# ViT tower kernel: the third channel's loads of the first sixteen image chunks move from SyncE's DMA queue to ScalarE's

## The reference, cut to what matters

```python
patches = X.reshape(B, C, N_PATCHES, PATCH, N_PATCHES, PATCH)
patches = patches.transpose(0, 2, 4, 1, 3, 5).reshape(B, N_PATCHES * N_PATCHES, IN_D)
tokens = jnp.einsum('bpi,hi->bph', patches, W) + b
...
h = _L0_tok_ref(x, ...)
h = h + _L0_attn_ref(_layernorm(h), ...)     # 512 positions at a time share weights and a moving average
h = h + _L0_ffn_ref(_layernorm(h), ...)      # each expert takes its 1024 best tokens
```

## Time and profile before

| | us |
|---|---|
| median of 3 runs | 994.54 |
| lowest, highest | 993.32, 994.76 |
| the profiled execution | 988.4 |
| its span, first to last instruction | 986.6 |
| TensorE busy | 756.6 (77% of the span) |
| ScalarE busy | 446.5 (45%) |
| VectorE busy | 556.1 (56%) |
| GpSimd busy | 477.7 (48%) |

### The profile page before, as it was taken

The page is one execution under the profiler, slowest core; times in us unless marked ns, Lnnn a source line. Parts: engine busy times, 40 slices in busy tenths (PEclk is TensorE's granted clock), DMA queues, the critical chain, the costliest instruction groups (busy, mean ns, idle before and its releaser), DMA issues.

```text
span 986.6 us, 9758 instructions
## 1 busy us (share of the span) xinstructions
PE 756.6 (77%) x2896; PEld 396.9 (40%) x2896; DVE 556.1 (56%) x1238; ACT 446.5 (45%) x730; POOL 477.7 (48%) x488
## 2 busy tenths in 40 slices
PE   0168489999999999999999995625128899788771
PEld 0123235544544554454445543414114455344330
DVE  0210157778778877877787777592687543231110
ACT  0634357656665775666566522321253132222220
POOL 2233444555545554645555322261110768888885
PEclk9778789999999999999999996856556799899896
DMA  9699998898889889888988111000010233343432
GB/s 224 155 207 212 199 208 203 195 217 192 207 196 218 195 206 218 198 191 200 217 191 197 49 31 34 21 12 11 22 14 1 47 53 63 63 66 63 66 38 27
DMA packets 135681, 126.39 MB, mean 128 GB/s; under 512 B 17605, under 2 KB 126013, under 8 KB 135501
## 3 DMA queue, kind: packets, MB, share of 16 engines
q1 hardware_dynamic: 113600, 91.27, 40.1%
q0 software_dynamic: 19488, 33.51, 18.0%
q10 hardware_dynamic: 2540, 0.99, 0.5%
HBM read 87.99 MB, written 12.98 MB: 102 GB/s over the span
## 4 chain that ended last, share of the span: by engine, by line
PE 25%; DVE 24%; POOL 20%; issue 15%; DMA 8%; ACT 5%; SPq 2%; ACTq 1%; DVEq 0%; POOLq 0%
PE bank L1352 10%; POOL out L620 9%; POOL XS L610 6%; DMA XS<-in_x 5%; DVE Y L966 4%; PE bank L1450 3%; DVE stats L916 3%; DVE O L908 3%; DVE XR L908 2%; DVE QT L1041 2%; ACT XS L819 2%; POOL rsB L492 2%; PE bank L1435 2%; PE bank L1481 2%; SPq L421 2%
## 5 line engine op out<-in xcount | busy, mean ns | idle before, releaser
L1352 PE MATMUL bank<-XS,WT 126*128 126x512 f32 (+1 forms) x608 | 313.2, 651 | 33.9 <-DMA XS<-XS 33.9
L801 ACT ACTIVATE XS<-XS 84x1152 f32<-84x1152 f32 (+1 forms) x192 | 187.6, 1027 | 34.7 <-DMA XS<-in_x 32.5
L1352 PEld LDWEIGHTS bank<-XS,WT 126*128 126x128 f32 (+1 forms) x608 | 113.2, 195 | 169.7 <-issue 168.8
L567 POOL COPY XS<-XS 84x1152 f32<-84x1152 f32 x64 | 89.0, 1390 | 82.1 <-DMA XS<-in_x 79.1
L620 POOL DMA_INDIRECT out<-XS x64 | 103.3, 1614 | 26.6 <-issue 18.6
L580 POOL DMA_DIRECT2D XS<-XS x128 | 71.3, 560 | 56.0 <-PE bank L1352 41.1
L610 POOL DMA_INDIRECT XS<-token_rows,XS x64 | 65.0, 1016 | 47.8 <-DVE XS L1244 28.6
L966 DVE TENSOR_TENSOR_SCAN Y<-qdec,XT 128x512 f32<-128x512 f32 (+1 forms) x68 | 78.5, 1175 | 8.4 <-ACT XT L688 8.4
L848 ACT ACTIVATE XS<-bank,VT 128x512 f32<-128x512 f32 x64 | 44.0, 687 | 66.8 <-PE bank L1562 66.8
L1562 PE MATMUL bank<-XS 128*128 128x512 f32 x128 | 69.5, 693 | 1.4 <-ACT XS L688 0.8
L972 DVE SCALAR_TENSOR_TENSOR ET<-Y,ema_c,ET 128x512 f32<-128x512 f32 (+1 forms) x68 | 61.7, 907 | 1.8
(11 more groups left out here) (236 smaller groups left out, 1289.3 us busy)
## 6 DMA issues: line engine op xcount, KB each, us to landing
XS<-in_x SPq DMA_DIRECT2D x192, 392.0 KB
XS<-XS POOLq DMA_DIRECT2D x128, 189.0 KB, 7.6
out<-O SPq DMA_DIRECT2D x16, 256.0 KB, 6.7
token_rows<-XR SPq DMA_DIRECT2D x16, 256.0 KB, 6.9
XS<-in_L_ffn_W SPq DMA_DIRECT2D x16, 256.0 KB, 3.1
XS<-in_L_tok_W SPq DMA_DIRECT2D x1, 1176.0 KB, 9.3
XS<-token_rows,XS POOLq DMA_INDIRECT x65, 2.6
out<-XS POOLq DMA_INDIRECT x64
```

The costliest lines, as they stand in the source:

```text
L567: pool.tensor_copy(ST[0:ROWS, n % 2, :, :, :].rearrange("p m j r -> p m r j"), px[:, :, :, PASSES:PATCH])\
L801: ins = act.activation(area(slice(0, ROWS), k // 4, piece, m0, m0 + CCOL // 2).rearrange("p m j r -> p m r j"), px[:, :, :, REST * piece:m ...
L1352: ins = pe.matmul(TOK[half][:, :], WT[rows, t, :], area(rows, half, t // REST)[:, :, t % REST, :], start=(t == 0), stop=(t == PASSES - 1))
```

## The change

SyncE issues only channels 0 and 1 of chunks 0 to 15 (`SHARED` is 16), and all three channels of the later ones. ScalarE issues channel 2 of chunks 0 to 15: chunk 0's ahead of all its small loads, chunks 1's and 2's behind them, and chunk `n + 3`'s right behind the last piece of its copy of chunk `n` (for `n` from 0 to 12), after waiting for `copied(n)` and `staged(n)`. The semaphores and their counts stay. The two helpers that build the access patterns move out of SyncE's function.

```diff
+        SHARED = 2 * CHUNKS
...
             def load_chunk(n):
 
                 if n < CHUNKS * NP:
-                    for c in range(C):
+                    for c in range(C - 1 if n < SHARED else C):
                         sp.dma_start(raw(n, c), rows_of(n % CHUNKS, n // CHUNKS, c)).then_inc(load[n % RING].sem, 16)
...
+            def load_last(n):
+
+                act.dma_start(raw(n, C - 1), rows_of(n % CHUNKS, n // CHUNKS, C - 1)).then_inc(load[n % RING].sem, 16)
+
+            load_last(0)
             for v, row, n in vectors:
...
             act.dma_start(lnb[:, :], bass.AP(ln_b.tensor, 0, [[0, 128], [1, D]])).then_inc(c_loaded.sem, 16)
+            for n in range(1, RING):
+                load_last(n)
...
                 if piece == C - 1:
                     ins.then_inc(copied.sem, 1)
+                    if n + RING < SHARED:
+                        act.wait_ge(*copied.done(n))
+                        act.wait_ge(*staged.done(n))
+                        load_last(n + RING)
```

More of the change, by code:

```diff
@@ L406, in run, with rows_of, raw @@
                 iteration(NP, ((None, group(NP - 1, 1)),), False, False)
+        def rows_of(k, hy, c):
+            return x[CHUNK * k:CHUNK * k + CHUNK, c, ds(hy * PATCH, PATCH), :].rearrange("b p w -> p b w")
+        def raw(n, c):
+            return RAW[c:ROWS:C, n % RING, :].rearrange("p (b w) -> p b w", b=CHUNK)
+        SHARED = 2 * CHUNKS
         @block.sync
         def _(sp):
[L411 to L415, removed]
             def load_chunk(n):
                 if n < CHUNKS * NP:
-                    for c in range(C):
+                    for c in range(C - 1 if n < SHARED else C):
                         sp.dma_start(raw(n, c), rows_of(n % CHUNKS, n // CHUNKS, c)).then_inc(load[n % RING].sem, 16)
```

## The result

| | before | after |
|---|---|---|
| median, same chip in turn (10 executions each) | 993.39 us (991.54 to 995.22) | 988.42 us (986.33 to 990.83) |
| ratio, 95% interval | | 0.9946 (0.9933 to 0.9959) |
| profiled execution, its span | 988.4, 986.6 us | 987.64, 985.9 us |

The change makes the kernel 5.0 us faster (993.39 - 988.42), 0.54%. The forecast was -3.0 us. The direction was right and the size was not: 988.42 us lies in the range of 985.5 to 997.0 and outside the 989.5 to 992.5 of the forecast case. Whether it came there by that rival's mechanism is what the runs have to say.

What follows compares the result with a forecast made beforehand. Loads bound the opening, which ends when chunk 15 arrives, and computing bounds what follows. Prologue -1.0 and stream -2.0, all else 0, sum to -3.0: 994.5 to 991.5 us, range 985.5 to 997.0.

Steps and rivals of the forecast that it cites:

- the forecast case: Whole kernel: earlier start plus part of the two-queue gain in the stream, 989.5 to 992.5 us, chance 0.38.
- that rival's mechanism: Opening stream: pixels gain from two queues as the constants' mixture did, or every byte does; below 989.5 us, chance 0.14.
- the prediction's signs of being wrong: Opening: chunk spacing 7.6 us or more, restart gated by something other than chunk 15's copy, or ScalarE issues delaying another engine.
- ScalarE's issues: Prologue and chunk copies: sixteen issues, 13 behind copies at 1.1 us each, hidden in ScalarE's idle time; price 0, at most 0.6.
- SyncE's issues worth 0: SyncE's load queue: sixteen issues fewer, at 0.81 or 1.63 us; the queue being full, issuing doesn't limit, so worth 0.
- The extras at 0: GpSimd's small moves, sharing DMA engines with two load queues: 8.0 us to landing against 8.9 with one, so 0.
- ScalarE held in the prologue: Rival, prologue: a full queue holds ScalarE's issues of chunks 1 and 2, delaying its start; 998.5 us, chance 0.08.
- The stream, -2.0: Loads of chunks 3 to 15: two queues move pixels faster than one; somewhat under half of 5.2 us, so -2.0.
- the 13% of the earlier trace: Opening DMA: 252 GB/s with two queues at 12 to 16 us against 222 with one; perhaps only the shape's.
- Full mixing: Rival, opening stream: pixels gain 5.2 us, or every byte 7.8, giving 988.3 down to 985.7; chance 0.14.
- Count what chunk 15 gains or loses one to one: After 139.4 us no more waiting for loads, so chunk 15's shift passes whole to the kernel's end.
- The prologue, -1.0: Start: 0.23 MB fewer pixels move before the last constant, 0.9 us at 252 GB/s, say -1.0; bounds -1.6 and +2.

Runs made afterwards that it cites:

- e4: Changed kernel, but of odd chunks among 0 to 15 ScalarE issues channels 1 and 2, so each queue carries half; 988.49 us, ratio 0.9940 to the kernel before.
- f2: Changed kernel, but all of chunk 1 is loaded by SyncE; 987.99 us, ratio 0.9948 to the kernel before.
- f4: Changed kernel, but ScalarE issues channel 2 of all 64 chunks instead of 16; 988.07 us, ratio 0.9949 to the kernel before.
- e2: Kernel before with only the stream part: ScalarE issues channel 2 of chunks 3 to 15, SyncE all of 0 to 2; 990.38 us, ratio 0.9960.
- m1: Only the 192 pixel loads into eight buffers, everything else of the kernel left out, all issued by SyncE; 357.99 us.
- m2: Only the 192 pixel loads into eight buffers, everything else left out, every second one issued by ScalarE, the others by SyncE; 329.31 us.
- e3: Kernel before with four resultless matmuls ahead of TensorE's wait for the first relu, so TensorE isn't idle there; 992.23 us, ratio 0.9985 to the kernel before.
- e1: Kernel before with only the prologue part: channel 2 of chunks 0 to 2 on ScalarE, the stream stays with SyncE; 996.05 us, ratio 1.0009.
- e6: Changed kernel, but GpSimd copies chunks 1 and 2 only after the constants are finished; 985.25 us, ratio 0.9955 to the kernel before on its chip.
- e9: Changed kernel with nine resultless matmuls on TensorE ahead of its wait for chunk 11's extras; 984.43 us, ratio 0.9952 to the kernel before on its chip.
- f1: Changed kernel with thirteen resultless matmuls on TensorE ahead of its wait for chunk 11's extras; 988.57 us, ratio 0.9953 to the kernel before.
- f3: Changed kernel with chunk 1 loaded wholly by SyncE and thirteen resultless matmuls ahead of TensorE's wait for chunk 11's extras; 989.28 us, ratio 0.9962.

## Why the prediction was right in direction and short in size

**Right.** The bound and its end in the kernel before: chunk 15's arrival set the restart, and all gains before it are one thing, the stream's rate. In the change this holds only just, as said below; in e4 and f2 the relu waits for VectorE instead, which is one of the prediction's signs of being wrong. ScalarE's issues: 13 at 0.82 us (819, 820 and 845 ns are the shortest, the median and the longest), `XT` at 124.39 against 124.04 and nobody late for it. SyncE's issues worth 0; its median fell from 1.63 to 0.84 us and nothing followed from that. The extras at 0, about: a median of 7.9 us to landing from 50 to 140 us against 8.4 before, and the wait for them 35.6 us in three against 33.9 in two. The same 4.65 MB took 22.5% of the engines' time in that window against 23.9%, some 1.3 us less, which is no term of the prediction either. ScalarE held in the prologue: the two issues took 4.03 us, inside the 9.66 spare. From the second relu on equal distances, until the last copy of a chunk.

**The stream, -2.0: the term was too small.** Chunk 15 came 3.56 us earlier in the change, 3.09 in f4 and 2.62 in e2. The question behind it was whether the 13% of the earlier trace rows were the second queue's or the shape's. m1 and m2 answer: with one shape, two queues move 245 / 224 = 1.09 times as much, so some two thirds of it were the queue's. Put into the prediction's own sum this gives 0.80 MB a chunk at 245 instead of 224 GB/s, 0.31 us, or 3.7 over 12 chunks. That it meets the measured 3.56 so well is partly luck: of the 3.7 some 3.1 would fall before 120 us (75 of 90.9 us), 4.8 were won there, and 1.1 were lost again. I had taken somewhat under half of 5.2 for want of a row; the kernel of loads alone would have been that row. Full mixing's 5.2 was not reached, and not only for the rate: that loss lies in the dry stretch, where ScalarE's order, through `QKT`, holds chunk 15's load.

**"Count what chunk 15 gains or loses one to one": this step failed.** It took the restart as a point that shifts. But the 4.40 us of standing before it also cost the clock, and a row says so: line 1418 took 2.07 us. With 3.4 us gained the wait disappears whole, because its start moved too. Before, the pass's matmuls ended at 130.05 + 4.96 = 135.01 and TensorE stood from there; after, they end at about 136.1. The pass's first four matmuls took 6.34 us instead of 5.51, which left it 0.2 us late in spite of its earlier start, and its last five waited for a VectorE step (line 1055) that took 1.35 us beside GpSimd's copy of chunk 14 (129.17 to 130.47), where it took 0.29 before: the collision of the prologue once more. VectorE's input (135.28), the relu (135.31 to 135.94) and the end of the pass now nearly coincide, so by these rows an earlier chunk 15 alone would gain next to nothing more. e3 gives the price of the clock without any gain in the stream: 2.2 us. So the second relu is 5.7 us earlier: 3.4 by the stream and 2.3 by the clock, and 0 by the prologue, where the forecast had 2.0, nothing and 1.0. This is why 988.42 landed in "full mixing's" band while the stream itself gained less than that rival says: the rival's number came true without its mechanism. That 988.42 lies inside the stated range is partly luck too, as the clock is not among the reasons that the range was built from.

**The prologue, -1.0: the bytes were right, the gain was lost behind them.** The constants came 1.01 us earlier, as worked out; GpSimd's copy of chunk 1 took it all back on VectorE (+0.34 at the first copy), e1 shows it to be worth nothing, and e6 shows the collision and also that its removal only moves the loss to the extras.

**From the trace to the total.** The traces differ by 5.7 us from 167 to 549 us, and the medians by 5.0 (ratios times 993.39: 4.1 to 6.7). The two profiled executions differ by only 0.7 us in span. What lies behind the second relu is code that the change doesn't touch, and it took 818.4 us after (985.9 - 167.53) and 813.4 before. In the other kernels it falls into two groups by chip: 817.2 to 820.9 on the chips whose kernel before has a median of 994.27 or 993.39, and 814.5 (e6) and 813.1 (e9) on the one with 988.93. The profiled before, 988.4 us with a tail of 813.4, looks like an execution on a chip of the second kind, set beside a median of 994.5 from the first; on which chip it ran isn't on record. For a change in the opening the landmarks inside the trace tell more than the two spans.

## What to carry to other kernels

When the DMA engines are 98% busy, ask what rate they move at, not only how busy they are; if the loads are of small pieces from one queue, measure them alone from one and from two. When a wait in front of TensorE goes, price both its length and the clock of the matmuls behind it: the row's own duration (2.07 against 1.12 us) shows whether there is something to gain. And when a load is made to arrive later "because nobody waits for it", look at which engine handles it on arrival and who works beside that engine then; here it cost as much as the earlier constants gave.

## What the runs showed of the hardware

- A busy share of 98% is not a rate: 224 GB/s from one hardware queue and 245 from two (m1 and m2, one execution each), with 896-byte pieces on 28 partitions and nothing else running. Why the engines do better with two queues wasn't tried.
- In e9 the first four matmuls of a pass took 6.31 us behind a gap of 3.25 us, which followed 7.89 us of work, and in the change 6.34 behind 10.96 us; in f1, with no gap, they took 4.07. The price isn't fixed: the same four took 5.51 us in the kernel before behind 11.57 us, and 5.51 in f4 behind 12.45. At the restart, the matmul took 2.07 us behind a gap of 4.40 us and 2.00 behind 2.35 (e1), 1.12 to 1.13 behind gaps of 0.60 to 1.14 (f4, f1, f3, e9), and 1.12 in e3, where four matmuls stood in the gap.
- A VectorE copy of 0.51 us and one of 1.23 became 1.50 and 2.62 beside GpSimd's copies of 84 x 1152 numbers, and a 0.17 us step 1.19; held apart (e6) they took 0.49 and 1.23 and 0.17.
- With the loads of one chunk on two queues the chunks complete unevenly. GpSimd's copies of chunks 10, 11 and 12 start at 95.75, 105.50 and 111.51 us in the change, 9.75 and 6.01 apart, where the stream's mean is 7.3; in the kernel before the same copies start 7.9 and 8.0 apart. I read that as ScalarE's queue moving channel 2 of later chunks while SyncE's still owes the others; no run was made for it alone.
